# Reordering one group's steps on TensorE, ScalarE and VectorE in a fused cross-attention and mixture-of-experts block

## The reference, cut to what matters

```
x = layernorm(x)                                   # then g_x, b_x; context: layer norm, g_c, b_c
q, k, v = xn @ Wq, cn @ Wk, cn @ Wv                # 16 heads of 64, so 1024 columns each
attn = softmax(q k^T / 8) ;  a = (attn @ v) @ Wo
x = x + tanh(g_xattn) * a
h = layernorm(x) ; logits = h @ router_w           # 14 experts, the best one is taken
hid = gelu(h @ w1[e] + b1[e]) ; y = (hid @ w2[e] + b2[e]) * softmax weight of e
out = x + tanh(g_ffn) * y
```

## Time and profile before

| | us |
|---|---|
| median of 3 runs | 847.01 (844.67 to 847.43) |
| the profiled execution's own time | 842.3 |
| its span, first to last instruction | 840.6 |

### The profile page before, as it was taken

One profiled execution on the slowest core, in us unless ns is written; L12 is line 12 of the kernel. 1 busy time (PEld: TensorE's weight loads), 2 busy tenths in 40 slices (PEclk: granted clock), 3 DMA queues, 4 the chain that ended last, 5 costly groups with the idle time before them and its releaser, 6 DMA issues.

```text
span 840.6 us, 34275 instructions
## 1 busy us (share of the span) xinstructions
PE 762.6 (91%) x12698; PEld 694.0 (83%) x12699; DVE 579.5 (69%) x1518; ACT 573.5 (68%) x1172; POOL 477.3 (57%) x1038
## 2 busy tenths in 40 slices
PE   6899999999999999999999999999999996776675
PEld 6689988888888888888888888888888885665665
DVE  5257777777777777777777777777777865454544
ACT  3667877777777777777777777777777654344442
POOL 2545466665666666665555556666666645455545
PEclk8989999999999999999999999999999998899977
DMA  4840011000001101000110001100000052433330
GB/s 121 242 120 20 20 33 32 30 30 30 30 30 31 34 30 36 30 30 30 33 36 31 30 30 32 34 30 30 20 22 22 28 177 99 140 113 99 104 90 24
DMA packets 52308, 45.82 MB, mean 55 GB/s; under 512 B 14726, under 2 KB 47783, under 8 KB 52250
## 3 DMA queue, kind: packets, MB, share of 16 engines
q1 hardware_dynamic: 45770, 32.23, 13.7%
q0 software_dynamic: 5536, 12.80, 4.4%
q10 hardware_dynamic: 944, 0.01, 0.1%
HBM read 28.15 MB, written 15.48 MB: 52 GB/s over the span
## 4 chain that ended last, share of the span: by engine, by line
PE 80%; issue 5%; another core or an unknown queue 2%; ACT 2%; DVE 1%; ACTq 0%; POOL 0%; DMA 0%; DVEq 0%; POOLq 0%
PE psJ L960 11%; PE psJ L961 10%; PE psJ L962 9%; PE psS L1019 9%; PE psO L1059 8%; PE psT L1084 7%; PE psM L1093 3%; PE psM L1094 3%; PE psO L1245 3%; PE psM L1101 3%; PE psM L1236 2%; PE psT L1236 1%; PE psM L971 1%; PE psM L1145 1%
## 5 line engine op out<-in xcount | busy, mean ns | idle before, releaser
L521 POOL TENSOR_TENSOR probs<-probs,row_inv 128x1024 f32<-128x1024 f32 x63 | 120.0, 1905 | 48.7 <-DVE row_inv L1487 47.9
L684 ACT ACTIVATE KT<-psJ 128x512 f32<-128x512 f32 x128 | 76.3, 596 | 51.6 <-PE psJ L962 49.1
L1019 PE MATMUL psS<-KT,QT 64*64 64x64 f32 x4032 | 89.9, 224 | 15.3 <-issue 13.3
L1482 DVE TENSOR_REDUCE row_sum<-probs 128x16 f32<-128x1024 f32 x63 | 76.5, 1215 | 36.2 <-ACT probs L736 36.2
L1019 PEld LDWEIGHTS psS<-KT,QT 64*64 64x64 f32 x4032 | 74.3, 136 | 31.8 <-issue 27.3
L730 ACT ACTIVATE PTs<-psT 128x512 f32<-128x512 f32 x126 | 74.8, 593 | 31.1 <-PE psT L1084 31.0
L684 ACT ACTIVATE V<-psJ 128x512 f32<-128x512 f32 x128 | 73.1, 598 | 26.1 <-PE psJ L962 22.7
L1446 DVE TENSOR_REDUCE row_max<-psS 128x16 f32<-128x1024 f32 x63 | 74.9, 1189 | 21.1 <-PE psS L1019 21.1
L1495 DVE TENSOR_TENSOR OT_l<-psO,OT_h 128x1024 fp32r<-128x1024 f32 x60 | 73.2, 1221 | 18.5 <-ACT OT_h L723 18.5
L960 PE MATMUL psJ<-CT_h,Wk_h 96*128 96x256 f32 x256 | 77.8, 304 | 3.9 <-ACT QT L684 3.8
L736 ACT ACTIVATE probs<-probs 128x1024 f32<-128x1024 f32 x63 | 66.6, 1056 | 20.0 <-DVE probs L1453 19.9
(11 more groups left out here) (297 smaller groups left out, 2178.2 us busy)
## 6 DMA issues: line engine op xcount, KB each, us to landing
V<-rows_by_expert SPq DMA_DIRECT2D x42, 129.0 KB
QT<-rows_by_expert SPq DMA_DIRECT2D x35, 129.0 KB
x_in<-in_x_dram SPq DMA_DIRECT2D x32, 128.0 KB, 2.1
x_res<-in_x_dram SPq DMA_DIRECT2D x32, 128.0 KB, 2.1
c_in<-in_ctx_dram SPq DMA_DIRECT2D x32, 96.0 KB, 2.2
KT<-w_sb SPq DMA_DIRECT2D x16, 128.0 KB
rows_by_expert<-pad_row SPq DMA_DIRECT2D x1, 1806.0 KB, 11.9
w_sb<-in_L_ffn_w_dram SPq DMA_DIRECT2D x1, 1792.0 KB, 8.5
```

Of the source, the lines that this page charges most:

```text
L521: pool.tensor_tensor(pr, pr, row_inv[:, p.k % 2, :].unsqueeze(2).to_broadcast([P, 16, SEQ]), ALU.mult).then_inc(s_norm, 1)
L684: act.activation(dst, psJ[n % 2][:, :], ACT.Copy).then_inc(s_jobev, 1)
L1019: last = pe.matmul(psS[64 * c:64 * c + 64, col:col + SEQ], QT[part, p.par(), 2 * g + c, tok], KT[part, p.par(), 2 * g + c, tok], start=Tru ...
L1482: dve.tensor_reduce(row_sum[:, :], pr, AX.X, ALU.add).then_inc(s_sum, 1)
```

## The change

Three lists of calls are put in another order; no call is added or removed.

- TensorE, even step: `post_a` goes from behind job 1 to ahead of job 0, and `probs_T(p, 0)` from behind `post_a` to behind `router`. Jobs 0 to 3 then stand in a row. Odd step: `post_b` goes from between jobs 10 and 11 to ahead of job 10.
- ScalarE, even step: `values_high` goes from ahead of job 0's copy to behind job 5's, and `expo` from behind job 1's copy to behind job 3's.
- VectorE, even step: `sums` goes from the end to ahead of `places` and `values_low`.

```
@@ ScalarE, even step
-                    values_high(p)
                     job(p, 0)
                     job(p, 1)
                     if p.fixed and p.s == 0:
                         norm_in(p)
-                    expo(p)
                     job(p, 2)
                     job(p, 3)
+                    expo(p)
                     probs_out(p, 0)
                     job(p, 4)
                     job(p, 5)
+                    values_high(p)
                     route_exp(p)
@@ TensorE, odd step
                     probs_T(p, 0)
+                    post_b(p)
                     job(p, 10)
-                    post_b(p)
                     job(p, 11)
@@ TensorE, even step
                     value_sums(p)
+                    post_a(p)
                     job(p, 0)
                     job(p, 1)
-                    post_a(p)
-                    probs_T(p, 0)
                     job(p, 2)
                     job(p, 3)
                     router(p)
+                    probs_T(p, 0)
                     job(p, 4)
                     job(p, 5)
@@ VectorE, even step
                     route_hot(p)
+                    sums(p)
                     places(p)
                     values_low(p)
-                    sums(p)
```

## The result

| | before | changed |
|---|---|---|
| median of 4 runs each, us | 846.59 (844.67 to 847.43) | 833.23 (829.95 to 834.49) |
| profiled execution / its span, us | 842.3 / 840.6 | 832.4 / 830.7 |
| ratio | 1 | 0.984 (0.981 to 0.988) |

The changed kernel is faster by 13.4 us (9.9 between the two profiled executions); the forecast was 3.1, and the range ended at 836. The page of the changed kernel has these lines, to be read against the earlier trace rows: the clock, the chain by engine, the page's group of the small matmuls of `scores`.

What follows compares the result with a forecast made beforehand. TensorE's matmul sequence plus its standstills was taken as the bound. A group's +0.32 - 0.37 = -0.05 us gave -1.4 over 28 even steps, the first steps -1.7: total -3.1, 843.9 us, range 836 to 853.5.

Steps and rivals of the forecast that it cites:

- the even half: TensorE from value sums to odd scores, 8.66 us: +0.17 - 0.41 + 0.44 + 0.12, so +0.32 us a group (0.20 to 0.45).
- the wait of 0.26 for the bank: TensorE, jobs 0 to 3 in a row: job 2 waits 0.26 us (0.20 to 0.30) for job 0's copy.
- `probs_T(p, 0)` behind `router`: TensorE, even step: four transposes at 0.11 us each in the new place add 0.44 us (0.40 to 0.50).
- `probs_T(p, 1)`: TensorE, even step: waits for `probs_out(p, 0)`, now behind job 3's copy and `expo`; 0.12 us late (0 to 0.2).
- the odd half: TensorE from odd scores to value sums, 11.84 us: end set by `send`; -0.37 us a group (-0.10 to -0.47).
- The first steps: Steps 0, 2 and 4, counted apart from the 28 groups: together -1.7 us (-2.4 to -0.5).
- C: Rival: no `probs_T(p, 1)` wait, odd half gives 0.47, clock does not fall in the third slice (3 us); 836.7 us; chance 0.15.
- the 0.44 us by which VectorE, and with it the second indirect DMA, comes earlier: Odd step: with `sums` ahead of `places`, `scores_max`, `weight`, `prep`, `split_in` and `send` all come 0.44 us earlier.
- The allowance of 0.07 for more matmuls left over: Even scores: 22 to 28 matmuls left after the stop instead of 22, taking 0.07 off the 0.44 us gain.
- the hold-up: GpSimd's indirect DMA in `send` holds up TensorE's instruction supply until some 1.4 us after its start, starving small matmuls.
- B: Rival: the scores still stop at the same 42nd matmul, a place in the instruction stream; +5.3 us, 852.3 us; chance 0.25.
- D: Rival: the two halves cancel and the first steps give little; 847 us; chance 0.15.

Runs made afterwards that it cites:

- sums_only: Kernel before with only VectorE's part of the change (`sums` ahead of `places`): 822.8 us, 0.976 on the first chip; 779.7 us, 0.998 on the third.
- weight_first: Changed kernel with VectorE's `weight` ahead of `scores_max` in the odd step: 784.8 us, 1.008 on the second chip; 783.9 us, 1.005 on the fourth.
- before_send_first: Kernel before with GpSimd's `send` ahead of `split_in` in the odd step, first chip: 817.9 us, 0.972.
- after_third: Changed kernel, unchanged, apparently its third run, on the fourth chip: 780.2 us, 0.999.
- before_again: Kernel before, unchanged, run again with a profile on the third chip: 780.0 us, 0.998.
- sums_send_first: Kernel before with VectorE's `sums` ahead of `places` and GpSimd's `send` ahead of `split_in`, second chip: 781.5 us, 1.003.

## Why the prediction was right in direction and too small

Right: the even half. +0.25 us in these rows, +0.24 in the mean, where I said +0.32 (0.20 to 0.45). Job 2's second matmul stands 311.85 - 311.36 = 0.49 us behind job 1's last, as read from the earlier trace rows: the wait of 0.26 for the bank, and `post_a` added the 0.17. `probs_T(p, 0)` behind `router` cost 0.38, below its bounds of 0.40 to 0.50: from job 3's last matmul to job 4's second it is 314.09 - 313.02 = 1.07 us, where it was 0.69. `probs_T(p, 1)` follows `probs_out` (315.42; ScalarE's copy at 314.78 takes 0.59) by 0.05 us, and the wait costs 0.10 where I said 0.12: from job 5's last matmul to job 6's second it is 1.21 us (315.14 to 316.35) instead of 1.11 (322.02 to 323.13). So the terms were 0.17 - 0.41 + 0.38 + 0.10 = +0.24. That a switch between jobs and transposes is nearly free holds, and `sums_only`, which leaves them as they were, has the shorter group.

Right: the mechanism of the odd half. Its end is set by the second DMA, and `sums` ahead of `places` brings that forward. The first steps: -2.0 us, forecast -1.7; job 4 in step 0 waits 1.38 us (1.4 said). In step 2 `probs_T(p, 1)` waits 1.65 us where I said some 0.5. C's item on the clock did not come true: the digit of the third slice rose from 8 to 9 tenths, but the stretch at 1.2 GHz was not gone. It lay at 39.5 to 46.3 us, after the wait of 2.34 us in step 0, and lies at 56.4 to 59.8, after that of 1.65; the third slice's mean went from 0.90 to 0.92 only, the second's from 0.94 to 1.00.

Wrong: one term, the 0.44 us by which VectorE, and with it the second indirect DMA, comes earlier against the odd scores. It was 0.79, and this took the time out of the range. `scores_max` starts 1.23 us behind the odd scores instead of 1.77: -0.54, of which I had 0.44. From its start to L1579's it took 0.07 longer. And L1579 took 0.23 us instead of 0.61, so that `xf` follows 0.20 us behind its start instead of 0.52: -0.32, which I had not counted. -0.54 + 0.07 - 0.32 = -0.79. The forecast moved `scores_max`, `weight` and `prep` by one and the same amount, so it took their durations as properties of the instructions. L1579's was not one: it was the rest of GpSimd's `normalise`. When VectorE moves by 0.5 us against GpSimd, the overlap goes, and it gives back more than the shift. `weight_first` shows the same with the other sign, 1.74 us.

The Trainium skill, "SBUF — State Buffer", section "Who interferes with whom", has that rule: a `tensor_scalar` of VectorE can enter a two-port mode, which takes an exclusive lock on the port pair shared with GpSimd, and the one that comes second blocks until the other's instruction is done. The rows agree: L1579 ended 0.02 to 0.03 us behind `normalise` in those groups of the kernel before and of `weight_first`, in which they overlapped. The two instructions ahead of it, a reduction (L1575) and a reciprocal (L1577), also ran under `normalise` in the kernel before, at 306.74 and 306.94, and took 0.17 us each, as they do in `weight_first` at 314.21 and 314.42, where the first stands ahead of `normalise`.

The allowance of 0.07 for more matmuls left over was about right: in the mean the distance from the second DMA to the value sums grew from 1.85 to 1.95 us. So the odd half gave 0.70 us and not the full 0.79 (said: 0.37, with 0.47 as the bound), and the group +0.24 - 0.70 = -0.46 where I said -0.05. 28 x -0.46 - 2.0 = -14.9, beside 14.6 measured for the first part. Of the 11.8 us by which this differs from the forecast of 3.1, some 28 x 0.33 = 9.2 are the odd half, 28 x 0.08 = 2.2 the even half, and 0.3 the first steps.

Two sums of the prediction are off in themselves. C's own items, 0.20 for the even half and 0.47 for the odd one, make -0.27 a group and not -0.2, so its time is 834.7 and not 836.7. That is nearer to what was measured, but 3 us of it are the clock item, which did not come. And the upper bound of the group is +0.45 - 0.10 = +0.35 and not +0.30.

Wrong in another way: the premise that the hold-up is a property of this kernel. It was there in the profile that I had, and the change does gain 13 us under it. On three other chips the same kernel took 779 to 781 us, and on the two of them on which the change ran it gives 0.1 to 0.2%, no more than the kernel before differs from itself (0.2%). That the changed kernel is faster at all is tied to the chip of the first trace, and the prediction had no row that could have told this.

Of the rivals, B (the stop stays in its place) is refuted by `before_send_first`; C is nearest in time, but of its three items only the odd half came, and larger than its 0.47: the wait of `probs_T(p, 1)` was not 0, and the clock did fall. In D the halves cancel, and they did not. On the later chips, where `scores` don't wait for the DMA, D's outcome holds: even half 8.91 in after_third (311.98 less 303.07), odd half 10.67, and the group, 19.58 us, as long as in before_again (19.62) to 0.04 us.

## What to carry to other kernels

When a step is moved against another engine's, don't carry its duration along: ask which rows of it were longer than the same operation elsewhere, and whether a neighbour's instruction ended with them. A stop that nothing recorded ended is worth a row of its own in the other engines' timelines at that time; moving the suspect, and not the victim, is the experiment that settles it (one swap on GpSimd gave 24 us, more than the three reordered lists). And if a gain rests on such a stop, run both kernels on more than one chip before keeping the more complicated order.

## What the runs showed of the hardware that I had not expected

- The same kernel took 842 to 847 us on the first chip and in the first trace, and 779 to 781 us on three others, with the same durations of single instructions (L521 1.90, L564 1.0, L684 0.6 us) and the same DMA bytes. Against before_again some 27 us lie in the first part (last value sums at 680.97 against 654.11), most of it the hold-up, and some 34 in the expert part. Each chip was used in one set of runs only, so chip and hour can't be told apart; why they differ stays open.
- In the expert part GpSimd issues indirect DMAs as well (L620), and there too engines stand idle: TensorE's weight loads of L1245 had 12.5 us of idle time that nothing recorded ended, against 0.5, and VectorE waited 48.1 us ahead of L1889 against 12.0 (kernel before, first trace against third chip). That these stops follow those DMAs was not tested.
- In the first trace and on the first chip TensorE's small matmuls stopped, and the value sums behind them started 1.7 to 2.1 us behind the start of GpSimd's second indirect DMA, 1.05 us late a group in the kernel before. On the third chip, at the same distance, it was 0.1 us; on the second, in `weight_first`, with the DMA 0.04 us behind the scores, nothing (0.98 us from scores to value sums).
- One stop without a recorded end is left on the other chips in most variants, in the last value sums; here it ends 3.7 us behind the start of the last such DMA before it (651.83), and it is not explained. TensorE in before_again:

```profile
655.55 0.58 PE L1059 MATMUL psO<-PTs,V 64*64 64x64 f32 x24 [0.63 <-issue]
```

- On the first chip, `send` at the end of the odd value sums came with a ScalarE copy that started 1.8 us late in the changed kernel; on the second chip, with `sums_send_first`, it did not.
- A VectorE instruction of two elements a partition took 0.23, 0.61, 0.76 or 1.74 us, by how much of GpSimd's `normalise` was left.
